# Who issues the stores of y: ScalarE's queue or GpSimd, in a two-layer depthwise convolution

## The chip, the cores and the metric

The kernel runs on one core of a Trainium2 chip. The metric is the device time of one execution in microseconds (us). The kernel before takes 3320.15 us, the median of 3 runs (3318.07 to 3320.52).

## The reference

The input x has the shape 8 x 384 x 128 x 128 in float32. Two layers follow one another, and each adds to x a depthwise convolution of x after group normalisation with 32 groups of 12 channels:

```
x = x + conv3x3_depthwise(group_norm(x), k)            # pad 1
x = x + conv7x7_depthwise(group_norm(x), w_sym)        # pad 3
# group_norm: mean and variance of one image over the 12 channels of a group and all pixels
# w_sym: the mean of the weight and its three turns by 90 degrees
```

## The kernel before

**Tiling.** Work goes in steps. A step takes a chunk: 4 channels of 4 images, 128 x 128 pixels each, with the image row as partition and channel, image and column along the free side (1 MB in float32). Three chunks make a unit, which is one group of 12 channels of 4 images; that is what the statistics are taken over. There are 192 chunks. `walk` writes the steps out one after the other, from t = -5 to t = 197, for each engine by itself; engines meet at semaphores only. Nothing is planned: each engine executes its own list in the order in which `slot` writes it.

**What an engine does in step t.** Different stages of different chunks lie in one step:

- SyncE's queue (SP): the tap matrices, then `load` of chunk t+6 (four transfers of 256 KB, one for each image), then `gather_low` of chunk t-3 (eight transfers).
- VectorE (DVE): the statistics' last part (`finish`) when a unit begins, the addition of conv 2 to chunk t-5 (L443), four subtractions for the low parts of chunk t-3 (L465), the statistics of chunk t+4 (L474), the addition of conv 1 to chunk t (L492), and the copy L498 of 39 partitions by 8512 fp16 for chunk t-3.
- ScalarE (ACT): normalises chunk t-3 to Z (L524), then chunk t+1 in image order to H (L541, the high part) and Z (L544), with one `store` of chunk t-5 after each image, then squares chunk t (L567).
- GpSimd (POOL): `high_parts2` of chunk t-3 (four L625), `gather_high` of the same chunk (four transfers from SBUF to SBUF, L638), `low_parts1` of chunk t+1 (four subtractions, L646).
- TensorE (PE): conv 1 of chunk t (L718), conv 2 of chunk t-4 (L747).

**What ties them.** A number in fp32 is given to the matmuls as a high and a low fp16 part. For conv 2 the rows of the image are gathered into BT, in four windows of 36 or 39 rows: the high parts by GpSimd, the low parts by SP. The copy L498 waits for the four high transfers of its chunk (`high_gathered`) and conv 2 of the next step waits for the copy. L465 needs the results of L624 to L626 image by image (`hi_done`), L541 waits for L465 since both use the same Z, and L646 waits for L544. L625 of a new unit waits for the ten small steps of `finish` on VectorE.

**The place of a chunk in X.** X is a ring of 12 chunks. `load` of chunk n waits for the four stores of chunk n-12 (`stored`), and stands in SP's list in front of `gather_low` of the same step. The four stores of a chunk are issued one step earlier than the load that waits for them.

In what follows the three kinds of step are called A, B and C. In A a unit begins at chunk t-3, and `finish(1)` stands at the head of VectorE's step; B is the next step; C follows it and has `finish(0)` at its head.

Of the kernel before, what the change touches and what calls it, by code (L numbers as in the profile page):

```python
# [12 lines left out]
GC = 12  # L13
NI = 4
CC = 4
# [43 lines left out]
def conv_program(nc, x, k1_in, k2_in, out):  # L59
# [18 lines left out]
    with ExitStack() as ctx:  # L78
# [88 lines left out]
        def xs(n, img):  # L167

            c = n % CPU_
            return X[:, ring(n), c * CC:(c + 1) * CC, img, :]  # L170
# [18 lines left out]
        def wait_apart(eng, semaphore, value):  # L189


            eng.wait_ge(semaphore, value)
            if not isinstance(value, int):
                eng.sem_inc(passed, 1)
# [3 lines left out]
        def real(n):  # L198
            return 0 <= n < NCH
# [312 lines left out]
        @block.scalar  # L512
        def _(act):
            def normalise2(n, at):

                m = NI * at(n)
                rb = RB[:, 1, (n // CPU_) % 2]
                for img in range(NI):

                    if real(n + 3):  # L520
                        act.wait_ge(lo_done[0], m + 3 * NI + img + 1)
                    else:
                        act.wait_ge(lo_done[1], m - NI + img + 1)
                    nc.scalar.activation(Z[:, img, :].rearrange("p (c w) -> p c w", c=CC), xs(n, img),  # L524
                                         ACT.Identity, bias=rb[:, 1, img:img + 1],
                                         scale=rb[:, 0, img:img + 1]).then_inc(normed[1], 1)

            def normalise1(n, img, at):

                m = NI * at(n)  # L530
                rb = RB[:, 0, (n // CPU_) % 2]
                if img == 0:
                    if n == 0:
                        act.wait_ge(zeroed, 9)
                    if n >= 2:
                        wait_apart(act, conv1_done, at(n) - 1)
                if real(n - 4):
                    act.wait_ge(lo_done[1], m - 4 * NI + img + 1)
                elif n > 0:
                    act.wait_ge(lo_done[0], m - NI + img + 1)  # L540
                nc.scalar.activation(part(H1, n, 0, img, O1, P1), xs(n, img), ACT.Identity,  # L541
                                     bias=rb[:, 1, img:img + 1],
                                     scale=rb[:, 0, img:img + 1]).then_inc(hi_done[0], 1)
                nc.scalar.activation(Z[:, img, :].rearrange("p (c w) -> p c w", c=CC), xs(n, img),  # L544
                                     ACT.Identity, bias=rb[:, 1, img:img + 1],
                                     scale=rb[:, 0, img:img + 1]).then_inc(normed[0], 1)

            def store(n, img, at):

                c, half = n % CPU_, (n // CPU_) % HALVES  # L550
                ch0 = (at(n - n % GCH) // GCH) * GC + c * CC
                if img == 0:
                    wait_apart(act, out_done, at(n) + 1)
                dst = out[half * NI + img, bass.ds(ch0, CC), :, :].rearrange("c h w -> h c w")
                act.dma_start(dst, xs(n, img)).then_inc(stored[n % BODY], 16)

            def take_root(layer, u):
                act.wait_ge(fin[layer], u * FIN + 4)
                nc.scalar.activation(TMP[:, layer, 3], TMP[:, layer, 2], ACT.Sqrt).then_inc(root[layer], 1)  # L559

            def square(n, at):

                for img in range(NI):
                    act.wait_ge(y_done, NI * at(n) + img + 1)
                    if n > 0 or img >= 2:
                        act.wait_ge(squared, NI * at(n) + img - 1)
                    nc.scalar.activation(DUMP[:, img % 2].rearrange("p (c w) -> p c w", c=CC), xs(n, img), ACT.Square,  # L567
                                         accum_out=SS[:, n % CPU_, img, 1:2]).then_inc(squared, 1)

            def slot(t, at):  # L570
                n = t - 3
                if real(n) and n % CPU_ == 0:
                    take_root(1, at(n) // CPU_)
                n = t + 1
                if real(n) and n % CPU_ == 0:
                    take_root(0, at(n) // CPU_)
                n = t - 3
                if real(n):
                    if n % CPU_ == 0:
                        act.wait_ge(fin[1], (at(n) // CPU_) * FIN + FIN)  # L580
                    normalise2(n, at)
                n = t + 1
                if real(n) and n % CPU_ == 0:
                    act.wait_ge(fin[0], (at(n) // CPU_) * FIN + FIN)
                for img in range(NI):
                    if real(t + 1):
                        normalise1(t + 1, img, at)
                    if real(t - 5):
                        store(t - 5, img, at)
                if real(t):  # L590
                    square(t, at)

            walk(act, slot)


        @block.gpsimd
        def _(pool):
            g = nc.gpsimd
            g.memset(v1_sb.bitcast(F32), 0.0).then_inc(zeroed, 1)
            g.memset(diag, 0.0).then_inc(zeroed, 1)  # L600
            pool.wait_ge(zeroed, 2)
            for k in range(2):
                d = diag[:, k * G:(k + 1) * G]
                g.affine_select(out=d, in_=d, compare_op=ALU.not_equal, fill=1.0, base=0, pattern=[[-1, G]],
                                channel_multiplier=1).then_inc(zeroed, 1)
            g.memset(onesg, 1.0).then_inc(zeroed, 1)
            g.memset(ONES1[:], 1.0 / P).then_inc(zeroed, 1)
            g.memset(ONES2[:], 1.0 / (GC * P * W)).then_inc(zeroed, 1)

            for whole in (BAND1[:], H1[:]):  # L610
                g.memset(flat32(whole), 0.0).then_inc(zeroed, 1)
            for whole in (H2[:], v2_sb, BAND2[:]):
                g.memset(flat32(whole), 0.0).then_inc(zeroed, 1)
            pool.wait_ge(zeroed, 12)

            def high_parts2(n, at):

                u = at(n - n % CPU_) // CPU_
                wait_apart(pool, fin[1], u * FIN + FIN)
                if n >= 2:  # L620
                    wait_apart(pool, high_gathered[n % 2], ((at(n) - n % 2) // 2) * HIGH_LANDED)
                    wait_apart(pool, low_gathered[n % 2], ((at(n) - n % 2) // 2) * LOW_LANDED)
                rb = RB[:, 1, (n // CPU_) % 2]
                for img in range(NI):  # L624
                    g.tensor_scalar(part(H2, n, 0, img, O2, P2), xs(n, img), rb[:, 0, img:img + 1],  # L625
                                    rb[:, 1, img:img + 1], ALU.mult, ALU.add).then_inc(hi_done[1], 1)  # L626

            def gather_high(n):

                q = n % 2  # L630
                if n < 2:
                    pool.wait_ge(blocks_zeroed, 1)
                else:
                    pool.wait_ge(conv2_done, n - 1)
                pool.wait_ge(hi_done[1], NI * n + NI)
                for b in (0, 2, 1, 3):
                    lo_row, hi_row, r0 = window(b)
                    pool.dma_start(BT[r0:r0 + hi_row - lo_row, q, b, :, :],  # L638
                                   H2[lo_row:hi_row, q, 0, :, :]).then_inc(high_gathered[q], 16)

            def low_parts1(n, at):

                for img in range(NI):
                    wait_apart(pool, normed[0], NI * at(n) + img + 1)
                    wait_apart(pool, hi_done[0], NI * at(n) + img + 1)
                    g.tensor_tensor(part(H1, n, 1, img, O1, P1), Z[:, img, :].rearrange("p (c w) -> p c w", c=CC),  # L646
                                    part(H1, n, 0, img, O1, P1), ALU.subtract).then_inc(lo_done[0], 1)

            def slot(t, at):
                if real(t - 3):  # L650
                    high_parts2(t - 3, at)
                    gather_high(t - 3)
                if real(t + 1):
                    low_parts1(t + 1, at)
                if t == 1:

                    pool.wait_ge(vectors_stored[1], 16)
                    g.memset(flat32(BT[:]), 0.0).then_inc(blocks_zeroed, 1)

            walk(pool, slot)  # L660


# [110 lines left out]
```

## Time and profile before

| what | value |
|---|---|
| median of 3 runs | 3320.15 us |
| the profiled execution's own time | 3324.27 us |
| its span | 3322.5 us |
| TensorE's granted clock, mean | 0.962 |
| busy share of PE, DVE, ACT, POOL | 86%, 83%, 65%, 64% |
| mean DMA rate | 214 GB/s |

The profile is of one execution on the chip. Busy time is counted by engine; instructions that issue a transfer from SP or ACT don't count as busy and stand under SPq and ACTq, while those of GpSimd do (POOL L638), since its cores write the descriptors. A line of the code names a group of instructions. The store on ACT is shown at L555, the load on SP at L248. "Idle before" is the time in which an engine had nothing to execute, with the instruction or transfer that ended it. Queue q1 is SP's, q10 ACT's and q0 GpSimd's.

### The profile page before, as it was taken

The page shows a single profiled execution, that of the slowest core. Times are in us where ns is not written, and L with a number is a line of the kernel's source. Part 1 is how long each engine was busy: PE and PEld are TensorE (multiplying, and loading weights), DVE is VectorE, ACT ScalarE, POOL GpSimd, SP SyncE. Part 2 cuts the span into 40 slices and gives each one's busy share as a digit, 9 for nine tenths or more (in the row PEclk, how much of TensorE's full clock was granted, in tenths as well). Part 3 has the DMA queues.
Part 4 walks back from the last instruction along what each step waited for, and adds up shares of the span by engine and source line. Part 5 has one row for each costly group of instructions (what it writes and reads, how often), then busy time and mean ns, then how long its engine had stood idle before and what let it go on. Part 6 is the DMA issues. An engine that isn't in the chain of part 4 may idle for free.

```text
span 3322.5 us, 76555 instructions
## 1 busy us (share of the span) xinstructions
PE 2873.4 (86%) x28676; PEld 1813.7 (55%) x28676; DVE 2768.8 (83%) x5180; ACT 2176.0 (65%) x3969; POOL 2127.9 (64%) x2321
## 2 busy tenths in 40 slices
PE   0468989998999999999999899999989989999996
PEld 0245555565555555555555555555555555555553
DVE  3567888889888889888988988888898888898885
ACT  1355676676667667667666766666766766676672
POOL 3245666766766666666676676676667667666763
PEclk9889999999999999999999999999999999999998
DMA  2699888888888888888888888888888888888866
GB/s 88 163 229 233 219 221 225 223 219 217 224 218 230 228 218 216 223 218 216 230 223 218 220 222 215 227 226 226 220 217 218 224 224 220 224 222 222 219 168 167
DMA packets 966522, 712.46 MB, mean 214 GB/s; under 512 B 102918, under 2 KB 904710, under 8 KB 966086
## 3 DMA queue, kind: packets, MB, share of 16 engines
q1 hardware_dynamic: 511494, 383.52, 45.4%
q10 hardware_dynamic: 405504, 201.38, 21.4%
q0 software_dynamic: 49152, 122.65, 16.0%
q8 instruction: 227, 3.72, 0.5%
q14 instruction: 145, 1.19, 0.1%
HBM read 259.73 MB, written 220.81 MB: 145 GB/s over the span
## 4 chain that ended last, share of the span: by engine, by line
DVE 49%; DMA 13%; issue 13%; POOL 10%; ACT 5%; PE 5%; SPq 4%; ACTq 1%; DVEq 0%; POOLq 0%
DMA BT<-H 12%; DVE X L492 9%; DVE H L465 9%; DVE BN L474 8%; DVE BT L498 8%; POOL H L625 7%; DVE X L443 4%; PE PS L747 3%; SPq L248 2%; PE PS L718 2%; POOL BT L638 2%; POOL H L646 2%; ACT Z L524 2%; ACT H L541 1%; DVE TMP L423 1%
## 5 line engine op out<-in xcount | busy, mean ns | idle before, releaser
L718 PE MATMUL PS<-H,BAND 128*128 128x512 f16 x6912 | 1609.2, 393 | 90.3 <-DMA BAND<-rows 72.2
L718 PEld LDWEIGHTS PS<-H,BAND 128*128 128x128 f16 x6912 | 1026.2, 151 | 628.5 <-issue 125.1
L747 PE MATMUL PS<-BT,BAND 118*32 118x512 f16 x21504 | 1245.8, 389 | 95.6 <-DMA BT<-H 40.8
L646 POOL TENSOR_TENSOR H<-Z,H 128x512 f16<-128x512 f32 x768 | 835.7, 1099 | 677.5 <-ACT Z L544 676.5
L747 PEld LDWEIGHTS PS<-BT,BAND 118*32 118x32 f16 x21504 | 767.3, 131 | 560.1 <-issue 200.3
L625 POOL TENSOR_SCALAR H<-X,RB 128x512 f16<-128x512 f32 x768 | 798.7, 1048 | 341.3 <-DVE RB L432 318.6
L541 ACT ACTIVATE H<-X,RB 128x512 f16<-128x512 f32 x768 | 618.8, 806 | 497.9 <-DVE H L465 425.3
L498 DVE COPY BT<-BT 39x8512 f16<-39x8512 f16 x192 | 465.0, 2422 | 296.1 <-DMA BT<-H 292.2
L524 ACT ACTIVATE Z<-X,RB 128x512 f32<-128x512 f32 x768 | 563.0, 804 | 105.7 <-DVE RB L432 83.5
L544 ACT ACTIVATE Z<-X,RB 128x512 f32<-128x512 f32 x768 | 615.5, 801 | 0.0
L567 ACT ACTIVATE DUMP<-X 128x512 bf16<-128x512 f32 x768 | 475.8, 620 | 132.7 <-DVE X L492 132.2
L638 POOL DMA_DIRECT2D BT<-H x768 | 465.9, 612 | 142.7 <-POOL H L625 101.8
L474 DVE BATCH_NORM_STATS2 BN<-X 128x6 f32<-128x512 f32 x768 | 472.9, 677 | 80.2 <-DMA X<-in_x 80.1
L492 DVE SCALAR_TENSOR_TENSOR X<-PS,SC,X 128x512 f32<-128x512 f32 x768 | 528.2, 742 | 4.2 <-PE PS L718 4.1
L465 DVE TENSOR_TENSOR H<-Z,H 128x512 f16<-128x512 f32 x768 | 505.8, 717 | 15.9 <-POOL H L625 11.0
L443 DVE SCALAR_TENSOR_TENSOR X<-PS,SC,X 128x2048 f32<-128x2048 f32 x192 | 451.4, 2351 | 14.4 <-PE PS L747 7.9
L559 ACT ACTIVATE TMP<-TMP 128x4 f32<-128x4 f32 x128 | 26.3, 205 | 383.5 <-DVE TMP L424 383.5
L690 PE MATMUL PS<-MQ,ONES 128*128 128x8 f32 x128 | 24.8, 266 | 138.4 <-DVE X L492 129.9
L567 ACT ACTIVATION_READ_ACCUMULATOR DUMP<-X 128x1 f32 x768 | 143.7, 187 | 0.0
L690 PEld LDWEIGHTS PS<-MQ,ONES 128*128 128x128 f32 x128 | 20.6, 202 | 165.4 <-issue 165.4
L683 PE MATMUL PS<-SS,ONES 128*128 128x24 f32 x128 | 26.4, 286 | 93.5 <-ACT DUMP L567 93.5
L683 PEld LDWEIGHTS PS<-SS,ONES 128*128 128x128 f32 x128 | 19.7, 194 | 122.7 <-ACT DUMP L567 120.7
(48 smaller groups left out, 503.0 us busy)
## 6 DMA issues: line engine op xcount, KB each, us to landing
X<-in_x SPq DMA_DIRECT2D x768, 256.0 KB, 5.0
out_y<-X ACTq DMA_DIRECT2D x768, 256.0 KB, 5.5
BT<-H POOLq DMA_DIRECT2D x384, 162.1 KB, 5.2
BT<-H POOLq DMA_DIRECT2D x384, 149.6 KB, 5.8
BT<-H SPq DMA_DIRECT2D x576, 99.8 KB
BT<-H SPq DMA_DIRECT2D x384, 62.3 KB
BT<-H SPq DMA_DIRECT2D x192, 83.1 KB
rows<-v_all SPq DMA_DIRECT2D x8, 1638.0 KB, 11.8
```

Source lines behind the costliest of these rows:

```text
L465: v.tensor_tensor(part(H2, n, 1, img, O2, P2), Z[:, img, :].rearrange("p (c w) -> p c w", c=CC), part(H2, n, 0, img, O2, P2), ALU.subtract ...
L474: v.bn_stats(BN[:, c, img, :], xs(n, img)).then_inc(bn_done, 1)
L492: v.scalar_tensor_tensor(xs(n, img), PA[:, :, img * W:(img + 1) * W], SC[:, 0, bass.ds(g, 1)], xs(n, img), ALU.mult, ALU.add, accum_out=SS ...
L498: v.tensor_copy(BT[AGAIN:AGAIN + WIN, n % 2, :, :, :].rearrange("p b c l -> p (b c l)"), BT[0:WIN, n % 2, :, :, :].rearrange("p b c l -> p ...
L524: nc.scalar.activation(Z[:, img, :].rearrange("p (c w) -> p c w", c=CC), xs(n, img), ACT.Identity, bias=rb[:, 1, img:img + 1], scale=rb[:, ...
L541: nc.scalar.activation(part(H1, n, 0, img, O1, P1), xs(n, img), ACT.Identity, bias=rb[:, 1, img:img + 1], scale=rb[:, 0, img:img + 1]).the ...
L544: nc.scalar.activation(Z[:, img, :].rearrange("p (c w) -> p c w", c=CC), xs(n, img), ACT.Identity, bias=rb[:, 1, img:img + 1], scale=rb[:, ...
L567: nc.scalar.activation(DUMP[:, img % 2].rearrange("p (c w) -> p c w", c=CC), xs(n, img), ACT.Square, accum_out=SS[:, n % CPU_, img, 1:2]). ...
L625: g.tensor_scalar(part(H2, n, 0, img, O2, P2), xs(n, img), rb[:, 0, img:img + 1], rb[:, 1, img:img + 1], ALU.mult, ALU.add).then_inc(hi_do ...
L646: g.tensor_tensor(part(H1, n, 1, img, O1, P1), Z[:, img, :].rearrange("p (c w) -> p c w", c=CC), part(H1, n, 0, img, O1, P1), ALU.subtract ...
L718: last = mm(PA[:, ch, :], band[:, j, ws, :], data[:, :, O1 - 1 + j:O1 - 1 + j + W], start=k == 0, stop=k == 3 * K1 - 1)
L747: last = mm(banks2(n)[b * BL:(b + 1) * BL, ch, :], band[:, j, :], rows, start=j == 0, stop=j == K2 - 1, tile_position=(0, b * BL))
```

## The change

The function `store` moves, word for word but for the engine, from ScalarE's block to GpSimd's. It is no longer called between the images of ScalarE's normalisation of chunk t+1, but four times in a row behind `low_parts1`, at the end of GpSimd's step. The wait for `out_done` goes with it.

```
@@ ScalarE
-            def store(n, img, at):
-                ...
-                if img == 0:
-                    wait_apart(act, out_done, at(n) + 1)
-                dst = out[half * NI + img, bass.ds(ch0, CC), :, :].rearrange("c h w -> h c w")
-                act.dma_start(dst, xs(n, img)).then_inc(stored[n % BODY], 16)
...
                     if real(t + 1):
                         normalise1(t + 1, img, at)
-                    if real(t - 5):
-                        store(t - 5, img, at)
@@ GpSimd
+            def store(n, img, at):
+                ...
+                if img == 0:
+                    wait_apart(pool, out_done, at(n) + 1)
+                dst = out[half * NI + img, bass.ds(ch0, CC), :, :].rearrange("c h w -> h c w")
+                pool.dma_start(dst, xs(n, img)).then_inc(stored[n % BODY], 16)
...
                 if real(t + 1):
                     low_parts1(t + 1, at)
+                for img in range(NI):
+                    if real(t - 5):
+                        store(t - 5, img, at)
```

## Rows read from the trace of the kernel before

**Rows 1.** Page, part 1: busy time, share of the span, instructions.

```profile
PE 2873.4 (86%) x28676; PEld 1813.7 (55%) x28676; DVE 2768.8 (83%) x5180; ACT 2176.0 (65%) x3969; POOL 2127.9 (64%) x2321
```

**Rows 2.** Waits: engine, line, releaser, total us, times, longest us.

```profile
POOL H L646 <- ACT Z L544: 676.5, 515, 72.1
...
POOL H L625 <- DVE RB L432: 318.6, 64, 12.9
DVE BT L498 <- DMA BT<-H: 292.2, 69, 7.9
```

**Rows 3.** Timeline of GpSimd: start us, us, operation, idle before.

```profile
1518.11 2.05 POOL L638 DMA_DIRECT2D BT<-H  x4 [0.56 <-POOL H L625]
1520.18 4.23 POOL L646 TENSOR_TENSOR H<-Z,H 128x512 f16<-128x512 f32 x4
1524.40 3.01 POOL L625 TENSOR_SCALAR H<-X,RB 128x512 f16<-128x512 f32 x4
...
1536.92 1.09 POOL L646 TENSOR_TENSOR H<-Z,H 128x512 f16<-128x512 f32 x1 [6.88 <-ACT Z L544]
...
1553.88 1.09 POOL L646 TENSOR_TENSOR H<-Z,H 128x512 f16<-128x512 f32 x1 [3.81 <-ACT Z L544]
...
1563.86 4.06 POOL L625 TENSOR_SCALAR H<-X,RB 128x512 f16<-128x512 f32 x4 [4.66 <-DVE RB L432]
1568.48 2.05 POOL L638 DMA_DIRECT2D BT<-H  x4 [0.56 <-POOL H L625]
...
1584.71 1.09 POOL L646 TENSOR_TENSOR H<-Z,H 128x512 f16<-128x512 f32 x1 [3.08 <-ACT Z L544]
```

**Rows 4.** Timeline of VectorE, the copies of the same steps.

```profile
1529.83 2.41 DVE L498 COPY BT<-BT 39x8512 f16<-39x8512 f16 x1 [6.08 <-DMA BT<-H]
...
1543.76 2.38 DVE L498 COPY BT<-BT 39x8512 f16<-39x8512 f16 x1
...
1559.06 2.38 DVE L498 COPY BT<-BT 39x8512 f16<-39x8512 f16 x1
...
1577.40 2.63 DVE L498 COPY BT<-BT 39x8512 f16<-39x8512 f16 x1 [3.28 <-DMA BT<-H]
```

**Rows 5.** All high gathers: duration ns min/median/max, first and last start us.

```profile
L638 POOL DMA_DIRECT2D BT<-H x768: 505/505/2706, 165.1 to 3295.6; - x192
```

**Rows 6.** Page, part 5: groups, busy us and mean ns of one.

```profile
L625 POOL TENSOR_SCALAR H<-X,RB 128x512 f16<-128x512 f32 x768 | 798.7, 1048 | 341.3 <-DVE RB L432 318.6
...
L638 POOL DMA_DIRECT2D BT<-H x768 | 465.9, 612 | 142.7 <-POOL H L625 101.8
```

**Rows 7.** Page, part 3: queue, packets, MB, share of 16 engines.

```profile
q10 hardware_dynamic: 405504, 201.38, 21.4%
q0 software_dynamic: 49152, 122.65, 16.0%
```

**Rows 8.** All stores: duration ns min/median/max, first and last start us.

```profile
L555 ACTq DMA_DIRECT2D out_y<-X x768: 378/477/3311, 207.4 to 3318.5; - x192
...
DMA to landing us min/median/max: 2.3/5.5/17.0
```

**Rows 9.** Timeline: a step in which the gather's issue meets the copy.

```profile
1626.14 4.06 POOL L638 DMA_DIRECT2D BT<-H  x4 [0.56 <-POOL H L625]
1626.24 2.37 DVE L498 COPY BT<-BT 39x8512 f16<-39x8512 f16 x1 [4.32 <-DMA BT<-H]
```

**Rows 10.** Timeline: a step A whose gather left after most store traffic.

```profile
2740.01 0.47 ACTq L555 DMA_DIRECT2D out_y<-X  x1
...
2742.39 2.06 POOL L638 DMA_DIRECT2D BT<-H  x4 [3.57 <-issue]
...
2750.05 2.47 DVE L498 COPY BT<-BT 39x8512 f16<-39x8512 f16 x1 [5.02 <-DMA BT<-H]
```

**Rows 11.** SP's waits for stores, and the first low gather of a step B.

```profile
SPq L248 <- DMA out_y<-X: 80.1, 44, 7.7
...
1537.10 0.77 SPq L237 DMA_DIRECT2D BT<-H  x1
```

More of the change, by code:

```diff
@@ L546, in normalise1 @@
                                      scale=rb[:, 0, img:img + 1]).then_inc(normed[0], 1)
-            def store(n, img, at):
-                c, half = n % CPU_, (n // CPU_) % HALVES
-                ch0 = (at(n - n % GCH) // GCH) * GC + c * CC
-                if img == 0:
-                    wait_apart(act, out_done, at(n) + 1)
-                dst = out[half * NI + img, bass.ds(ch0, CC), :, :].rearrange("c h w -> h c w")
-                act.dma_start(dst, xs(n, img)).then_inc(stored[n % BODY], 16)
             def take_root(layer, u):
@@ L639, in gather_high @@
                                    H2[lo_row:hi_row, q, 0, :, :]).then_inc(high_gathered[q], 16)
+            def store(n, img, at):
+                c, half = n % CPU_, (n // CPU_) % HALVES
+                ch0 = (at(n - n % GCH) // GCH) * GC + c * CC
+                if img == 0:
+                    wait_apart(pool, out_done, at(n) + 1)
+                dst = out[half * NI + img, bass.ds(ch0, CC), :, :].rearrange("c h w -> h c w")
+                pool.dma_start(dst, xs(n, img)).then_inc(stored[n % BODY], 16)
             def low_parts1(n, at):
```

## The prediction, made before the changed kernel was run

> **What bounds the kernel now.** I read the busy shares first [rows 1]: no engine is full, PE at 86% and DVE at 83%, while POOL, which gets the new work, has 3322.5 - 2127.9 = 1195 us of idle time, 6.2 us for each of 192 steps. So the second view is who waits for whom [rows 2]: 676.5 us of POOL's idle time is a wait for ScalarE in front of L646 and 318.6 us a wait for the statistics in front of L625. These are waits at certain places; work that is put elsewhere in POOL's step can only use them if what lies between may be late. And DVE waits 292.2 us, 69 times, almost once in three steps, for the high gather which POOL issues.
>
> The third view is POOL's timeline [rows 3] with DVE's copies [rows 4]. I cut one turn of three steps (A, B, C) into four pieces, each ended by something that the next one needs:
>
> 1. End of A's high gather issue (1518.11 + 2.05 = 1520.16) to B's first L646 (1536.92): 16.8 us. The gather lands, the copy starts at 1529.83, that is 9.7 us after the issue, and 7.1 us later (addition, L465, ScalarE) L646 can run. In the next turn it is 1570.53 to 1584.71 = 14.2 us, of which 6.9 for the landing.
> 2. B's first L646 to C's first (1553.88): 17.0 us, DVE and PE working with hardly a gap.
> 3. C's first L646 to A's first L625 (1563.86): 10.0 us. It ends with the statistics, 4.8 us behind the start of C's copy (1559.06).
> 4. L625, 0.56 idle, gather issue, to 1570.53: 6.7 us.
>
> Sum 50.4 us in this turn, 47.9 with the next turn's first piece, mean 49.2. The whole run says the same: gathers start from 165.1 to 3295.6 us [rows 5], 3130.5 / 191 x 3 = 49.2 us. The kernel is bound by this ring through POOL, DVE and the gather, and POOL has its slack inside it, not beside it.
>
> **What the change removes.** From ScalarE's queue 768 issues, median 477 ns [rows 8]. They lie beside its activations, and the ring's pieces wait for ScalarE only behind L465; I take 0 us for it. From the time of A's gather it takes the stores' traffic: in the code they stand between ScalarE's normalisations, beside A's gather. How much faster the gather lands without them, one step shows [rows 10]: ScalarE's last store was issued by 2740.5, the gather at 2742.39 to 2744.45, and the copy started at 2750.05, 5.6 us later instead of 6.9 or 9.7. So piece 1 could fall to 5.6 + 7.1 = 12.7 us if POOL kept pace. That is a gain of up to 15.5 (the mean of 16.8 and 14.2) - 12.7 = 2.8 us a turn.
>
> **What it adds on POOL: the price S of one store's issue.** POOL has no such instruction in this trace. Its gathers take 505 ns, median and minimum alike [rows 5], but a gather is 49152 / 768 = 64 packets and a store 405504 / 768 = 528 [rows 7]. Lower bound: 0.505 us, if the price does not grow with packets. Upper bound: 0.505 x 528 / 64 = 4.2 us, if it is all packets. ScalarE's queue writes the same 528 packets in 0.48 us, which speaks against the upper end, but that is a queue of another kind. I take S = 1.2 us, about twice the gathers' mean of 612 ns [rows 6], since that row is the same engine and the same kind of issue; four of them are 4.8 us a step.
>
> **The lock.** In [rows 9] the four issues take 4.06 us instead of 2.05, and they began 0.10 us before the 2.37 us copy L498: GpSimd's first issue lasted until the copy's end. The longest single one is 2706 ns [rows 5], 505 plus about a copy. So an issue that meets a copy waits for its end. The Trainium skill, SBUF — State Buffer, "Who interferes with whom", says that a copy on VectorE can take the port pair that it shares with GpSimd and that a transfer issued from GpSimd is then starved of descriptors; it speaks against this change, and the trace agrees with 4.06 us against 2.05. Today only few issues meet one. The stores will: they begin 4.2 us behind the start of L646. A's copy starts 5.6 us or more behind the gather's issue, so with L646 next (4.23 us) stores run from +4.2 to +9.0 and the copy falls in between. B's copy starts 6.8 us behind L646 (1536.92 to 1543.76), C's 5.2 us (1553.88 to 1559.06): both inside the same 4.2 to 9.0. I add 2.4 us to every step.
>
> **The sum, turn by turn.** POOL's own way through each piece, against what else holds it:
>
> 1. L646 4.2 + stores 4.8 + copy 2.4 + B's L625 3.0 + 0.56 + issue 2.05 = 17.0 us, over the 12.7 of the landing.
> 2. 4.2 + 4.8 + 2.4 + C's L625 4.2 (4 x 1048 ns, [rows 6]) + 0.56 + 2.05 = 18.2 us, over 17.0.
> 3. 4.2 + 4.8 + 2.4 = 11.4 us, over 5.6 + 4.8 = 10.4 of the landing and the statistics.
> 4. 6.7 us as before.
>
> Together 53.3 us instead of 49.2: 4.1 us a turn, 64 turns, +262 us. At the tail the last four stores cost 4 x (1.2 - 0.48) = 3 us once, within the rounding. 3324.27 + 262 = 3586 for the profiled execution; the median before lies 4 us lower, so 3582 us. POOL becomes the bound: 12 x 1.2 + 3 x 2.4 = 21.6 us are added to its turn, and the waits they use up are not that large.
>
> The wait for `out_done` costs nothing where it now stands: the addition L443 opens DVE's step, and L646 in front of the wait already needs what follows it.
>
> **Rivals.**
>
> *The issue is cheap, faster (0.14).* If S stays at 0.61, piece 1 is 14.7, piece 2 is 17.0 (DVE and PE hold it), piece 3 is 10.0, together 48.4: -0.8 x 64 = -51 us, 3269 us; with S = 0.505 it is 14.3 + 17.0 + 10.0 + 6.7 = 48.0, -77 us, 3243 us. For it: the bare 505 ns; against it: eight times the packets. It decides below S = 0.82: piece 1 is 4.2 + 2.4 + 3.0 + 0.56 + 2.05 = 12.2 and 4S, the others 33.7, and with 3.3 for 4S that is 49.2. The Trainium skill, DMA: Bandwidth & Descriptors, "Anatomy of one DMA", says of GpSimd's path that one "can emit a lot of descriptors before the incremental cost shows up"; by that this rival is right. No run here shows it for 528 packets.
>
> *No meeting with the copy, faster (0.04).* At S = 1.2 without the 2.4 us: 14.6 + 17.0 + 10.0 + 6.7 = 48.3, 3262 us. It decides below 0.9 us lost a step. Against it are the times of the copies above.
>
> *The issue is priced by packets, much slower (0.12).* S = 2 gives 53.3 + 12 x 0.8 = 62.9, 4197 us; S = 4.2 gives 89.3, 5886 us.
>
> *SP waits for the stores, slower still (0.10).* The stores leave by +11.4 us and land 5.5 us later [rows 8], at +17; then SP issues four loads (at least 2 us) before the step's low gathers, which today start at 1537.10, +16.9 behind A's gather [rows 11]. SP's 80.1 us of waiting for stores would grow, the low gathers come a few us late, and conv 2 waits for them. A guess of 2 us a step gives 3582 + 384 = 3966 us.
>
> *No difference (0.04).* S between 0.8 and 0.85, or traffic out of the way worth just what POOL loses: 3320 us.
>
> The forecast itself has 0.56, with S from 1.0 (16.2 + 17.4 + 10.6 + 6.7 = 50.9, 3429 us) to 1.45 (56.3, 3774 us).
>
> **Range.** 3250 to 4050 us: below it lies a part of the cheap rival, above it nearly all of the one priced by packets (S over 1.8). Faster by over 0.2% 0.18, within 0.2% 0.04, slower 0.78; 0.2%, 7 us, is about what a measurement of this kernel can tell from no change.
>
> **What the changed profile would show.** POOL's store line with its mean: 1.2 us wanted, with single ones of 3 us and more where a copy runs. POOL's busy time up by 768 x 1.2 + 192 x 2.4 = 1380 us to some 3500 us of a 3585 us span, PE's share down to 80%. POOL's waits for ScalarE and for the statistics nearly gone. The turn, gather to gather, 53 us. In A the copy within 6 us of the gather's issue. ScalarE waiting longer for DVE, and nothing won from its queue. The forecast is wrong if the mean issue is below 0.8 us, or if the stores cross no copy.

## The result, and the profile after

The changed kernel takes 3504.04 us (median of 4 runs, 3500.32 to 3507.05) against 3320.34 us of the kernel before: ratio 1.0554, 95% interval 1.0536 to 1.0572. That is slower, as forecast, and inside the range, 78 us under the 3582 us of the prediction.

First the page of the changed kernel: span, busy shares, GpSimd's queue, and the groups of GpSimd and of VectorE's copy. `store` is now L637, the high gather L627, the high parts L614, the low parts of conv 1 L644.

```profile
span 3505.2 us, 76555 instructions
...
PE 2926.2 (83%) x28676; PEld 1847.7 (53%) x28676; DVE 2851.2 (81%) x5180; ACT 2174.2 (62%) x3969; POOL 2907.8 (83%) x3089
...
q0 software_dynamic: 110592, 324.03, 33.3%
...
L614 POOL TENSOR_SCALAR H<-X,RB 128x512 f16<-128x512 f32 x768 | 895.3, 1174 | 68.3 <-DVE RB L432 41.6
...
L637 POOL DMA_DIRECT2D out_y<-X x768 | 761.3, 997 | 26.0 <-DVE X L443 26.0
L498 DVE COPY BT<-BT 39x8512 f16<-39x8512 f16 x192 | 483.1, 2516 | 361.3 <-DMA BT<-H 359.4
```

GpSimd's busy time is up by 779.9 us over [rows 1]. The stores' issues are 761.3 us, 4.0 us a step, where I had forecast 7.2. The other changes nearly cancel: the high parts take 96.6 us more (1174 ns each instead of 1048) and the gathers 62.4 us less (403.5 us instead of 465.9), both against [rows 6]. Then the two lines that give the price of one issue and of one gather (ns min/median/max):

```profile
L637 POOL DMA_DIRECT2D out_y<-X x768: 750/767/2942, 213.0 to 3499.3; - x192
```

```profile
L627 POOL DMA_DIRECT2D BT<-H x768: 505/512/2282, 163.1 to 3474.7; - x192
```

A store's issue is 0.75 to 0.77 us when nothing is in its way. The mean of 0.997 says what the meetings with the copy add to the stores: 0.23 us an issue, 0.92 us a step instead of the 2.4 that I had put. The gathers, first to last, give a turn of three steps of (3474.7 - 163.1) / 191 x 3 = 52.0 us, against 49.2 [rows 5].

The waits of the changed kernel, to be held against [rows 2] (one row of before that was not shown follows in a fence of its own):

```profile
ACT H L541 <- DVE H L465: 472.6, 119, 8.1
DVE BT L498 <- DMA BT<-H: 359.4, 137, 7.0
POOL H L644 <- ACT Z L544: 358.0, 372, 72.7
...
DVE H L465 <- POOL H L614: 56.3, 88, 4.3
...
POOL H L614 <- DVE RB L432: 41.6, 18, 12.6
```

```profile
DVE H L465 <- POOL H L625: 11.0, 18, 1.0
```

GpSimd's two waits fell from 995 to 400 us, so most of the new work did go into them. But VectorE's copy now waits 137 times for the gather instead of 69. The new 68 are not in steps A: in 55 turns from the middle of the run it waits in every step A with either kernel, and in the changed one also in 45 steps B and 21 steps C, for 60 and 15 us in all. The timeline of GpSimd in one turn, A at 1522.69 to 1536.71, then B, then C from 1552.79 (columns as in [rows 3]):

```profile
1522.69 4.06 POOL L614 TENSOR_SCALAR H<-X,RB 128x512 f16<-128x512 f32 x4
1527.36 2.10 POOL L627 DMA_DIRECT2D BT<-H  x4 [0.61 <-POOL H L614]
1529.47 4.23 POOL L644 TENSOR_TENSOR H<-Z,H 128x512 f16<-128x512 f32 x4
1533.65 3.06 POOL L637 DMA_DIRECT2D out_y<-X  x4
1536.75 5.13 POOL L614 TENSOR_SCALAR H<-X,RB 128x512 f16<-128x512 f32 x4
1542.49 2.09 POOL L627 DMA_DIRECT2D BT<-H  x4 [0.61 <-POOL H L614]
1544.60 2.33 POOL L644 TENSOR_TENSOR H<-Z,H 128x512 f16<-128x512 f32 x2
...
1552.79 5.16 POOL L614 TENSOR_SCALAR H<-X,RB 128x512 f16<-128x512 f32 x4
1558.56 2.10 POOL L627 DMA_DIRECT2D BT<-H  x4 [0.61 <-POOL H L614]
1564.21 1.09 POOL L644 TENSOR_TENSOR H<-Z,H 128x512 f16<-128x512 f32 x1 [3.55 <-ACT Z L544]
...
1574.45 4.56 POOL L614 TENSOR_SCALAR H<-X,RB 128x512 f16<-128x512 f32 x4
1579.62 2.09 POOL L627 DMA_DIRECT2D BT<-H  x4 [0.61 <-POOL H L614]
```

And VectorE's copies of the same turn:

```profile
1537.16 2.58 DVE L498 COPY BT<-BT 39x8512 f16<-39x8512 f16 x1 [4.22 <-DMA BT<-H]
...
1553.83 2.71 DVE L498 COPY BT<-BT 39x8512 f16<-39x8512 f16 x1 [2.58 <-DMA BT<-H]
...
1569.37 2.39 DVE L498 COPY BT<-BT 39x8512 f16<-39x8512 f16 x1
```

The four pieces of the ring are here 15.1 us (1529.46 to 1544.60), 19.6 us (to 1564.21), 10.2 us (to 1574.45) and 7.3 us (to 1581.71), 52.3 together. The piece that grew is the second, and the reader can see why: B's gather leaves at 1542.49, 13.0 us behind the end of A's gather issue, and B's copy waits for it. Before, it left 7.8 us behind it (1527.98, in the row below, against 1520.16), and B's copy at 1543.76 [rows 4] found it long landed. Of these 5.2 us the stores are 3.1. The other 2.1 are B's high parts, 5.13 us instead of 3.01 [rows 3]: the stores had pushed them under A's copy (1537.16 to 1539.74).

```profile
1527.98 2.06 POOL L638 DMA_DIRECT2D BT<-H  x4 [0.56 <-POOL H L625]
```

One turn is one sample. The means over 55 turns from the middle of either run, in us:

| piece | before | forecast | changed |
|---|---|---|---|
| 1, to B's first subtraction | 15.0 | 17.0 | 15.5 |
| 2, to C's first subtraction | 17.0 | 18.2 | 18.5 |
| 3, to A's first high part | 10.0 | 11.4 | 10.5 |
| 4, to the end of A's gather issue | 6.9 | 6.7 | 7.2 |
| the turn | 48.9 | 53.3 | 51.6 |

Over the same turns B's first subtraction no longer waits for ScalarE: before, GpSimd idled in front of it in all 55, 3.7 us in the mean, and in the changed kernel in 4. There piece 1 has become GpSimd's own way.

TensorE's granted clock is lower as well, 0.947 instead of 0.962 in the mean, and its matmuls of conv 1 take 403 ns instead of 393. That doesn't carry the loss: VectorE waits no longer for TensorE than before, for its two additions (L443 and L492) 9.8 us in all instead of 12.0.

### The profile page after: what moved, and what is told of

It is laid out like the page before. It is cut to its first block, busy times and chain, and to the rows that moved or that the text cites. A ratio compares the mean times of both kernels' runs of the same rounds, so it can differ in the third digit from the quotient of the medians.

```text
span 3505.2 us, 76555 instructions
## 1 busy us (share of the span) xinstructions
PE 2926.2 (83%) x28676; PEld 1847.7 (53%) x28676; DVE 2851.2 (81%) x5180; ACT 2174.2 (62%) x3969; POOL 2907.8 (83%) x3089
## 3 DMA queue, kind: packets, MB, share of 16 engines
q0 software_dynamic: 110592, 324.03, 33.3%
## 4 chain that ended last, share of the span: by engine, by line
POOL 32%; DVE 24%; DMA 14%; ACT 13%; issue 10%; PE 4%; SPq 2%; DVEq 0%; POOLq 0%; ACTq 0%
DMA BT<-H 14%; POOL H L614 13%; POOL out_y L637 9%; DVE BT L498 7%; POOL H L644 7%; ACT H L541 6%; DVE H L465 4%; ACT Z L544 4%; POOL BT L627 4%; ACT Z L524 3%; DVE X L492 3%; DVE BN L474 3%; PE PS L719 2%; SPq L248 2%; PE PS L748 2%
## 5 line engine op out<-in xcount | busy, mean ns | idle before, releaser
L719 PE MATMUL PS<-H,BAND 128*128 128x512 f16 x6912 | 1666.3, 403 | 111.7 <-DMA BAND<-rows 72.1
L644 POOL TENSOR_TENSOR H<-Z,H 128x512 f16<-128x512 f32 x768 | 828.9, 1093 | 363.1 <-ACT Z L544 358.0
L748 PEld LDWEIGHTS PS<-BT,BAND 118*32 118x32 f16 x21504 | 792.9, 131 | 555.8 <-issue 219.5
L614 POOL TENSOR_SCALAR H<-X,RB 128x512 f16<-128x512 f32 x768 | 895.3, 1174 | 68.3 <-DVE RB L432 41.6
L637 POOL DMA_DIRECT2D out_y<-X x768 | 761.3, 997 | 26.0 <-DVE X L443 26.0
L498 DVE COPY BT<-BT 39x8512 f16<-39x8512 f16 x192 | 483.1, 2516 | 361.3 <-DMA BT<-H 359.4
L558 ACT ACTIVATE DUMP<-X 128x512 bf16<-128x512 f32 x768 | 475.7, 620 | 182.7 <-DVE X L492 182.7
L465 DVE TENSOR_TENSOR H<-Z,H 128x512 f16<-128x512 f32 x768 | 499.4, 702 | 56.4 <-POOL H L614 56.3
L492 DVE SCALAR_TENSOR_TENSOR X<-PS,SC,X 128x512 f32<-128x512 f32 x768 | 528.2, 743 | 1.1 <-PE PS L719 1.1
L627 POOL DMA_DIRECT2D BT<-H x768 | 403.5, 531 | 128.2 <-POOL H L614 116.5
L443 DVE SCALAR_TENSOR_TENSOR X<-PS,SC,X 128x2048 f32<-128x2048 f32 x192 | 451.3, 2351 | 15.2 <-PE PS L748 8.7
```

Source lines behind the costliest of these rows:

```text
L465: v.tensor_tensor(part(H2, n, 1, img, O2, P2), Z[:, img, :].rearrange("p (c w) -> p c w", c=CC), part(H2, n, 0, img, O2, P2), ALU.subtract ...
L492: v.scalar_tensor_tensor(xs(n, img), PA[:, :, img * W:(img + 1) * W], SC[:, 0, bass.ds(g, 1)], xs(n, img), ALU.mult, ALU.add, accum_out=SS ...
L498: v.tensor_copy(BT[AGAIN:AGAIN + WIN, n % 2, :, :, :].rearrange("p b c l -> p (b c l)"), BT[0:WIN, n % 2, :, :, :].rearrange("p b c l -> p ...
L637: pool.dma_start(dst, xs(n, img)).then_inc(stored[n % BODY], 16)
L719: last = mm(PA[:, ch, :], band[:, j, ws, :], data[:, :, O1 - 1 + j:O1 - 1 + j + W], start=k == 0, stop=k == 3 * K1 - 1)
L748: last = mm(banks2(n)[b * BL:(b + 1) * BL, ch, :], band[:, j, :], rows, start=j == 0, stop=j == K2 - 1, tile_position=(0, b * BL))
```

## The experiments

Two theories stood against each other. The first is GpSimd's time: the issues sit in the ring. The second is lateness: the stores leave later, SP's loads wait for them and hold up the low gathers. Ratios are against runs of the kernel before on the same chip.

**Late stores without GpSimd.** ScalarE keeps the stores and issues them behind its squares.

```
                     if real(t + 1):
                         normalise1(t + 1, img, at)
-                    if real(t - 5):
-                        store(t - 5, img, at)
                 if real(t):
                     square(t, at)
+                for img in range(NI):
+                    if real(t - 5):
+                        store(t - 5, img, at)
```

> The stores stay on ScalarE's queue but leave at the end of its step, behind the four squares, which is about as late as GpSimd issues them in the changed kernel; GpSimd issues none. If GpSimd's time is the cause (four issues of 0.76 us a step and what the copy adds), the kernel is within 1% of 3320 us. If the lateness of the stores is the cause (SP's loads wait for them, and the low gathers stand behind the loads), it is 3450 to 3510 us, like the changed one, with SP's wait for stores near 600 us.

Measured: 3329.43 us, ratio 1.0020 (1.0007 to 1.0033). SP's waits of this kernel, and below them those of the changed one:

```profile
SPq L248 <- DMA out_y<-X: 617.9, 155, 11.9
```

```profile
SPq L248 <- DMA out_y<-X: 616.1, 177, 7.5
```

Both wait the same 617 us for stores, against 80.1 us before [rows 11], and only one of them is slow. SP had the time; lateness by itself costs 0.2%.

**GpSimd's time without the stores.** The kernel before, with six small transfers behind `low_parts1`.

```
+                if real(t - 5):
+                    for i in range(6):
+                        pool.dma_start(idle[:, (t - 5) * 24 + i * 4:(t - 5) * 24 + i * 4 + 4],
+                                       ONES1[0:36, 0:4]).then_inc(small, 16)
```

> The kernel before, with its stores on ScalarE between the images, and six added transfers of 36 x 16 bytes at the end of GpSimd's step, to a scratch tensor that nothing reads: 6 x 0.5 = 3.0 us of GpSimd's issue time a step, the same as four stores of 0.76 us, with next to no traffic. If GpSimd's time and its meeting with the copy are the cause, 3480 to 3530 us. If the stores' lateness is, within 0.5% of 3320 us.

Measured: 3474.25 us, ratio 1.0460 (1.0442 to 1.0477). Most of the loss comes back with no store moved, though the dose was larger than planned, 4.4 us a step (below) instead of 3.0. Half of it:

> As with the six small transfers on GpSimd, but three: 1.5 us a step instead of 3.0. Six cost 4.6%. If the cost grows in line with GpSimd's time, 2.3% or 3396 us; if the ring has slack for the first 1.5 us, within 0.5%; if it comes from meeting the copy, which three issues at that place meet as often as six, 4% or more.

Measured: 3410.26 us, ratio 1.0203 (1.0187 to 1.0219). It grows about in line; there is no free first microsecond. And about the same time without any descriptor:

```
+                if real(t - 5):
+                    for i in range(6):
+                        if t > 5 or i:
+                            pool.wait_ge(filled, (t - 5) * 6 + i)
+                        g.memset(IDLE[:], 0.0).then_inc(filled, 1)
```

> The kernel before with six memsets of a 128 x 512 scratch tile at the end of GpSimd's step instead of transfers: some 0.45 to 0.5 us each, about 3 us a step with the semaphore between them, no descriptors and no traffic. If what costs is GpSimd's time in the ring, 3450 to 3490 us, as with six small transfers. If it is the descriptors, 3320 to 3360 us.

Measured: 3520.46 us, ratio 1.0540 (1.0512 to 1.0568). The added instructions of the three kernels, in the order told (six small, three small, memsets):

```profile
L660 POOL DMA_DIRECT2D idle<-ONES x1152 | 838.0, 735 | 0.0
```

```profile
L660 POOL DMA_DIRECT2D idle<-ONES x576 | 427.6, 748 | 6.7 <-issue 6.7
```

```profile
L661 POOL MEMSET IDLE<- 128x512 f32 x1152 | 865.9, 752 | 55.3
```

Divided by 192 steps: 2.2 us a step cost 2.0%, 4.4 us 4.6%, 4.5 us of memsets (with 0.3 us idle before them) 5.4%; the change adds 4.0 us and costs 5.5%. A memset costs no less than an issue, so neither descriptors nor traffic are needed for the loss: GpSimd being occupied is enough. Two things these doses leave open. Bare, a small transfer takes 0.51 us and a memset 0.53 (medians), so the means above hold meetings with the copy too, and the doses don't part plain time from meetings. And the change costs more for each microsecond than any dose, 1.4% against 0.9 to 1.2%; what the rest is, no run shows.

**Another place on GpSimd.** The stores in front of `low_parts1`, in the idle time of steps B and C.

```
+                for img in range(NI):
+                    if real(t - 5):
+                        store(t - 5, img, at)
                 if real(t + 1):
                     low_parts1(t + 1, at)
-                for img in range(NI):
-                    if real(t - 5):
-                        store(t - 5, img, at)
```

> The changed kernel with the four stores on GpSimd in front of the subtractions L646 instead of behind them. In steps B and C GpSimd idles there for 3.5 to 6.9 us, so 3 us of issues are covered, they meet fewer copies, and the stores leave 4 to 5 us earlier; in step A the subtractions come 3 us later and with them TensorE's conv 1 of the next step. Both theories (GpSimd's time, late stores) want it faster than 3504 us: 3380 to 3450 us. If it is not faster, conv 1 behind the subtractions is the tighter path.

Measured: 3542.69 us, ratio 1.0663 (1.0644 to 1.0682): slower still, and both theories missed it. Nor is conv 1 the tighter path: VectorE waits for it 6.4 us in all. GpSimd now waits for VectorE's addition in front of the stores, 226.7 us in all, but then does without most of its wait for ScalarE (94.7 us instead of 358.0). The stores' mean issue is down to 767 ns, so they meet no copy any more; GpSimd's busy time is lower than in the changed kernel (2733.0 against 2907.8 us). What grew is VectorE's busy time, by 273 us to 3042.0 us, and 192 us of that are one instruction, L482, a product of 128 x 4 numbers that took 852 ns in the median before (ns min/median/max):

```profile
L482 DVE TENSOR_TENSOR TMP<-MQ x64: 161/4690/4741, 29.7 to 3400.2; 128x4 f32<-128x4 f32 x64
```

Its timeline in that kernel, with GpSimd's rows around it:

```profile
1516.23 3.05 POOL L637 DMA_DIRECT2D out_y<-X  x4
1519.15 4.64 DVE L482 TENSOR_TENSOR TMP<-MQ 128x4 f32<-128x4 f32 x1
1519.29 4.22 POOL L644 TENSOR_TENSOR H<-Z,H 128x512 f16<-128x512 f32 x4
1523.52 3.01 POOL L614 TENSOR_SCALAR H<-X,RB 128x512 f16<-128x512 f32 x4
```

L482 ends when the four subtractions of GpSimd do (1523.79 against 1523.51). In the kernel before the subtractions of that step have gaps of 0.3 us between them, and L482 gets through in 0.85 us. So a row of GpSimd's subtractions without gaps holds this instruction of VectorE until the row's end. The changed kernel has it as well: there 14 of the 64 last 2.9 us or more, and each ends with the last subtraction, as here:

```profile
2008.73 4.23 POOL L644 TENSOR_TENSOR H<-Z,H 128x512 f16<-128x512 f32 x4
2009.78 3.21 DVE L482 TENSOR_TENSOR TMP<-MQ 128x4 f32<-128x4 f32 x1
```

**SP's order.** In the changed kernel, and then in the kernel before, the low gather in front of the load (the two blocks of `slot` change places).

> The changed kernel with SP's gather of the low parts in front of the load of the same step, so that no low gather stands behind a load that waits for a store. If SP's 616 us of waiting for stores is the cause through the low gathers, 3350 to 3400 us. If GpSimd's time is, 3490 to 3520 us.

> The kernel before with SP's low gather in front of the load of the same step. With the stores on GpSimd this order took 1% off the changed kernel's time. If it undoes a cost of the late stores, it gives nothing here: within 0.3% of 3320 us. If it is better by itself, this one is 1% faster, 3287 us, too.

Measured: 3470.09 us, ratio 1.0446 (1.0429 to 1.0464), and 3312.16 us, ratio 0.9911 (0.9891 to 0.9932). The first lies in neither expected range. The order is worth 1% with either kernel; it does not undo a cost of the late stores. The second is faster than both kernels, and so is the next, with the late stores of ScalarE added:

> Stores on ScalarE at the end of its step, and SP's low gather in front of its load. Late stores alone gave +0.2% with SP waiting 618 us for stores, the order alone -0.9%. If SP's wait in front of the low gathers had eaten what the late stores give to A's gather (its copy came 7.0 instead of 7.8 us behind the issue, 0.8 us a turn or 50 us), this kernel is 1.5 to 2% faster than before, 3265 us. If the two just add, 0.7% faster, 3297 us.

Measured: 3315.83 us, ratio 0.9928 (0.9906 to 0.9950). The two about add; nothing was hidden behind SP's wait.

**One kind of step at a time.** GpSimd issues the stores only in steps A, B or C, ScalarE in the other two.

```
-                    if real(t - 5):
+                    if real(t - 5) and t % 3 != K:        # ScalarE; K = 0, 1, 2 for A, B, C
...
+                    if real(t - 5) and t % 3 == K:        # GpSimd, behind low_parts1
```

> Stores on GpSimd only in steps A, on ScalarE in B and C as before. Behind A's subtractions GpSimd has no idle time, so B's high parts and B's gather leave 3 to 5 us later; before, B's gather had 10.5 us until its copy and took 5.5 to land. If each step pays for its own issue time, 3375 us (a third of the loss of 184 us, 64 x 1 us); if the slack of B's gather covers it, within 0.5% of 3320 us and the loss sits in the next step.

> Stores on GpSimd only in steps B. They stand in front of C's high parts and C's gather, which had 8.8 us until its copy. If each step pays for its own, 3375 us; by the ring's pieces C is the step with the least slack of the two gathers that don't hold the copy, 3340 to 3400 us.

> Stores on GpSimd only in steps C, in front of the wait of 4.7 us for the statistics. Four issues of 0.76 us lie in that wait; one that meets the copy makes it 5 us, just beyond it. Within 0.5% of 3320 us by the ring's pieces; 3375 us if each step pays for its own.

Measured: A 3469.58 us, ratio 1.0376 (1.0352 to 1.0400); B 3459.27 us, 1.0351 (1.0330 to 1.0372); C 3456.77 us, 1.0341 (1.0321 to 1.0361). Each alone costs two thirds of the whole, so the costs don't add, and all three expectations, 3320 to 3400 us, were wrong. That A's stores don't find cover behind B's gather is again VectorE's L482 in part: its busy time there is 144.5 us instead of 52.1. C is the instructive one. GpSimd's wait for the statistics did cover the issues (28.7 us of it are left of 318.6), and yet the copy waits longer, as often as before but 5.7 instead of 4.2 us each time. Over 55 turns A's copy starts 9.2 us behind the end of its gather issue, against 7.8 in the kernel before:

```profile
DVE BT L498 <- DMA BT<-H: 390.4, 68, 9.7
```

The timeline of that kernel:

```profile
1508.46 4.85 POOL L648 DMA_DIRECT2D out_y<-X  x4
1513.44 4.56 POOL L625 TENSOR_SCALAR H<-X,RB 128x512 f16<-128x512 f32 x4
...
1518.60 2.10 POOL L638 DMA_DIRECT2D BT<-H  x4 [0.60 <-POOL H L625]
1518.84 1.04 ACTq L555 DMA_DIRECT2D out_y<-X  x1
...
1530.16 2.37 DVE L498 COPY BT<-BT 39x8512 f16<-39x8512 f16 x1 [6.31 <-DMA BT<-H]
```

C's stores leave at 1508 to 1513 and A's, from ScalarE, up to 1519.9: 2 MB of y in 11 us in front of A's gather or beside it, whose copy comes 9.5 us behind its issue. That the traffic in a heap is the cause fits, but no run separated it from the rest.

**The price of an issue.** Each store cut into two of two channels.

```
-                pool.dma_start(dst, xs(n, img)).then_inc(stored[n % BODY], 16)
+                for a in (0, CC // 2):
+                    dst = out[half * NI + img, bass.ds(ch0 + a, CC // 2), :, :].rearrange("c h w -> h c w")
+                    src = X[:, ring(n), c * CC + a:c * CC + a + CC // 2, img, :]
+                    pool.dma_start(dst, src).then_inc(stored[n % BODY], 16)
```

> The changed kernel with each store cut into two of two channels: the same bytes in 512-byte runs, 256 runs an issue instead of 512. If the price of an issue is mostly fixed (0.50 us for a gather of 36 to 39 rows, 0.75 us for 512 runs), a half store is 0.61 to 0.65 us and eight take 5 us, so GpSimd's step is 2 us longer and the kernel 3600 us or more. If the price is by bytes or runs, a half is 0.38 us and the kernel stays near 3504 us.

Measured, in one run: 3868.6 us, beside 3332.64 us of the kernel before. The issues:

```profile
L639 POOL DMA_DIRECT2D out_y<-X x1536: 710/713/2793, 213.4 to 3860.5; - x192
```

256 runs cost 0.71 us, 512 of them 0.75: between these two the price is fixed but for 0.04 us. The eight issues take 7.5 us a step (1432 us in all), and GpSimd's two waits for ScalarE and the statistics still hold 245 us, in the changed kernel 400. The 3.5 us a step over the changed kernel cost some 365 us, more than twice as much for each microsecond as the first four. It is one run on its own, with a granted clock of 0.904.

## Why the prediction was right, and where it was right by luck

**Direction and bound: right.** The loss is for the most part GpSimd's time inside the ring; the six small transfers and the memsets show it, with the stores untouched, and late stores alone cost 0.2%. Piece 1 became GpSimd's own way, as the sum had it.

**The price S: too high.** The forecast put 1.2 us, the runs show 0.75 to 0.77. Its own sign of being wrong, a mean issue below 0.8 us, is met by the bare issue and not by the measured mean of 0.997, which holds the meetings with the copy. The upper bound rested on packets, 528 for a store. On GpSimd's queue the store has (110592 - 49152) / 768 = 80 packets for its 262144 bytes, 3.3 KB in the mean, against 528 on ScalarE's; how many packets a transfer makes differs by queue, and the price does not go by the count: by the same division a small transfer has 32 packets and a gather 64, for 0.51 us each, half a store 48 for 0.71 and a store 80 for 0.75. The Trainium skill, DMA: Bandwidth & Descriptors, "Anatomy of one DMA", says that one can emit a lot of descriptors before the cost of more of them shows. The traces agree, with 0.71 and 0.75 us for 256 and 512 runs.

**The lock: there, but smaller, and in part elsewhere.** Stores meet the copy, and single ones last 2942 ns. But the forecast gave each step's stores a whole copy, 2.4 us, and it was 0.92 us a step: in steps like the shown A and B the four issues (3.06 and 3.05 us) had ended before the copy began (1536.71 against 1537.16, 1552.75 against 1553.83). In 55 turns they met it 20 times in A, 31 in B and 55 in C. Where the stores had ended, the high parts behind them often met it. B's did in 44 of these turns, in 24 before, and they take 5.0 us in the mean instead of 3.2; the sum had kept them at 3.0. B's gather issues gave some of that back: the copy met them in 45 of 55 turns before, which the prediction called few, and in none now, 2.1 us instead of 3.2.

**The sum: near by luck, since errors of both signs nearly cancel.** With the measured 3.98 us a step in place of 7.2 the forecast's own pieces give 4.2 + 3.98 + 3.0 + 0.56 + 2.05 = 13.8, then 17.0, 10.0 and 6.7, together 47.5 us: 1.7 us a turn less than before, or 3211 us. So the condition of the cheap rival (S below 0.82) came true and its time did not. What the sum lacked is the lock on the high parts, above, and the floor under the pieces, "what else holds it":

- Piece 2 was given 17.0 us as DVE's and PE's own. It has a third way through it: the stores of A, then B's high parts, B's gather, its landing, B's copy. In the shown turn that landing took 9.3 us (1544.58 to 1553.83) and, with what follows the copy, set the piece's end. Before, there were 13.7 us for it and it never showed as a wait. I priced POOL's way to the end of the gather's issue and forgot the landing behind it.
- Piece 1 had GpSimd's way right in kind: with the means measured over 55 turns it is subtractions 4.4 + stores 3.5 + high parts 5.0 + 0.6 + gather issue 2.1 = 15.6 us, and the piece takes 15.5. The landing under it was to be 5.6 us; A's copy started 7.7 us behind the issue in the shown turn and 7.2 in the mean, against 7.8 before. The single step of [rows 10] was no measure for the others.
- Piece 3 had a floor of 10.4 us in the sum and of 10.0 in the rivals; it was 10.0 before and is 10.5 now.
- VectorE's own time was taken as given. It grew by 82.4 us, from 2768.8 to 2851.2. The growth sits in three places for the most part: two small instructions of 128 x 4 numbers, L424 (25.8 to 62.6 us) and L482 (52.1 to 85.8), and the copy (465.0 to 483.1).

The last point can be held against the whole. VectorE's time is busy or idle, so a few differences to the kernel before should account for the difference of the spans; us, from the pages and the waits of each:

| kernel | span | DVE busy | copy L498 waits for the gather | L465 waits for GpSimd | these three together |
|---|---|---|---|---|---|
| changed | +182.7 | +82.4 | +67.2 | +45.3 | +194.9 |
| six small transfers | +150.5 | +133.3 | -28.0 | +48.2 | +153.5 |
| memsets | +191.2 | +114.6 | +33.9 | +48.1 | +196.6 |
| changed, gather first | +150.3 | +149.3 | -47.6 | +70.2 | +171.9 |
| stores on GpSimd in C only | +129.4 | -26.1 | +98.2 | +29.9 | +102.0 |

The three columns come within 28 us of the loss each time and trade with one another: where the copy waits less, VectorE's instructions are stretched more. In the kernel with the gather first B's copy waits for nothing in the 55 turns, and piece 2 is still 17.9 us, so the landing alone is not what makes it long. This is bookkeeping: it says where VectorE's time went, and not why. The spans are of single executions on different chips, and the kernel before takes some 20 us longer on the chips of the memsets and of the last row than on that of its trace. Which column grows seems to hang on how the two engines happen to fall together; that was not tested. How large the share of each would be if the other were gone stays open; it wasn't tried, since a copy or a product that leaves GpSimd alone would have been another instruction with another duration.

**The other rivals.** SP's wait for the stores grew from 80 to 616 us as that rival said, and the same wait in the first experiment cost 0.2%. The price by packets is out. ScalarE gained nothing from the issues that it lost, as forecast; its wait for VectorE is up by 47 us.

## What to carry to other kernels

GpSimd idled for 36% of the time here and was still part of the ring that sets the time. Before work is moved onto it, follow each thing that it issues to the end of its use, the landing of a transfer included, and ask how long that has before somebody waits; the idle time that lies elsewhere in the step is no cover. The cheapest test is a dose: add the expected time to the engine as something harmless, half of it and all of it, and read the slope before the real change is written. Here it gave 4.6 and 5.4% where the change cost 5.5%.

## What the runs showed of the hardware

- An issue on GpSimd took 0.51 us for 36 rows of 16 bytes, 0.71 us for 256 runs of 512 bytes and 0.75 us for 512 of them.
- VectorE and GpSimd hold each other up. A store's issue that met VectorE's copy took up to 2.9 us instead of 0.75, and the four high parts of a step 5.1 us instead of 3.0. A VectorE product of 128 x 4 numbers, 161 ns at its shortest, took 4.7 us beside four GpSimd subtractions without gaps, not the 1.1 us of one of them. With gaps of 0.3 us between them it took 0.85 us. A whole row of instructions, not one, was the unit in which VectorE waited.
